# A four-layer decoder with cross-attention and a composed MLP: the first norm's two loads on separate semaphores, two column products for four, and GpSimd's weight splits at another wait

## What is computed

```python
for i in range(4):                                   # x: 2048 tokens x 256
    h = layer_norm(x, ln1_g[i], ln1_b[i])            # (x - m) * rsqrt(v + eps) * g + b
    # heads 0-3: windowed softmax attention; heads 4-7: q = softmax(q), k = elu(k) + 1,
    # ctx = running sum over buckets of k^T v / sum(k), out = q @ ctx
    x = x + self_attention(h, Wq[i], Wk[i], Wv[i], Wo[i], bo[i])
    h = layer_norm(x, ln2_g[i], ln2_b[i])
    x = x + gelu(h @ W1[i] + b1[i]) @ W2[i] + b2[i]
x = layernorm(x0 + x)                                # x0: the input
x = layernorm(x + cross_attention(x, ctx_1024, Wq, Wkv, Wout, bout))
vals, idx = top_k(logits, 32)                        # twice, for fc1 and fc2, of 64 primitives
w = softmax(vals)
W = einsum('k,kir,kro->io', w, A[idx], B[idx])       # the composed weights
x = layernorm(x + gelu(x @ W_fc1) @ W_fc2)
```

## Time and profile before

| | us |
|---|---|
| median of 3 runs | 959.26 |
| lowest, highest | 958.53, 959.52 |
| the profiled execution, its own time | 958.49 |
| its span, first to last instruction | 956.3 |
| TensorE busy with products | 944.4 |
| VectorE busy | 673.6 |
| ScalarE busy | 611.8 |
| GpSimd busy | 480.2 |

### The profile page before, as it was taken

The page is one execution under the profiler, slowest core; times in us unless marked ns, Lnnn a source line. Parts: engine busy times, 40 slices in busy tenths (PEclk is TensorE's granted clock), DMA queues, the critical chain, the costliest instruction groups (busy, mean ns, idle before and its releaser), DMA issues.

```text
span 956.3 us, 21341 instructions
## 1 busy us (share of the span) xinstructions
PE 944.4 (99%) x8394; PEld 815.6 (85%) x8394; DVE 673.6 (70%) x1529; ACT 611.8 (64%) x1389; POOL 480.2 (50%) x381
## 2 busy tenths in 40 slices
PE   7999999999999999999999999999999999999998
PEld 4688888888888889888888888888997889998997
DVE  7796868677777868696777678776662776666445
ACT  4777777686776867777768677686856345444220
POOL 3437375456826472775466367816247224006453
PEclk9999999999999999999999999999999999999999
DMA  6231000001110000021000003000028696820001
GB/s 211 72 108 45 2 17 2 8 11 58 33 45 19 2 1 19 1 89 45 10 9 1 18 2 84 4 2 7 2 57 204 137 205 143 181 46 1 23 23 45
DMA packets 71582, 47.56 MB, mean 50 GB/s; under 512 B 44511, under 2 KB 68159, under 8 KB 71487
## 3 DMA queue, kind: packets, MB, share of 16 engines
q1 hardware_dynamic: 71487, 46.27, 18.9%
HBM read 44.16 MB, written 2.10 MB: 48 GB/s over the span
## 4 chain that ended last, share of the span: by engine, by line
PE 94%; DVE 3%; ACT 1%; issue 1%; DMA 0%; POOL 0%; SPq 0%; POOLq 0%; DVEq 0%; ACTq 0%
PE F L1460 21%; PE F L1614 19%; PE A L1460 16%; PE A L1802 5%; PE A L1795 5%; PE A L1559 4%; PE A L1955 4%; PE A L1517 3%; PE F L1474 2%; PE A L1576 2%; PE A L1474 2%; PE F L1453 2%; PE A L1550 1%; PE A L1453 1%; PE A L1533 1%; PE A L1526 1%
## 5 line engine op out<-in xcount | busy, mean ns | idle before, releaser
L1460 PE MATMUL F<-xt,w 128*128 128x512 f32 x864 | 217.8, 400 | 0.2 <-ACT scratch L1211 0.2
L475 POOL TENSOR_TENSOR ht<-scratch,ht 128x512 fp32r<-128x512 f32 x128 | 176.2, 1397 | 29.4 <-ACT ht L1214 27.9
L1460 PEld LDWEIGHTS F<-xt,w 128*128 128x128 f32 x864 | 157.6, 188 | 38.2 <-issue 3.0
L1614 PE MATMUL F<-w,ht 128*128 128x256 f32 x1536 | 188.8, 282 | 0.0
L1614 PEld LDWEIGHTS F<-w,ht 128*128 128x128 f32 x1536 | 182.8, 188 | 5.3 <-issue 4.6
L463 POOL TENSOR_TENSOR rstd<-var,minus_half 128x4 f32<-128x4 f32 x32 | 37.6, 1173 | 176.4 <-DVE var L611 175.8
L1211 ACT ACTIVATE scratch<-F,b_now 128x512 f32<-128x512 f32 x128 | 87.6, 684 | 36.6 <-POOL ht L475 19.0
L1460 PE MATMUL A<-wa,xt 128*128 128x512 f32 x372 | 89.8, 397 | 0.0
L470 POOL TENSOR_TENSOR x<-x,vec_f 128x1024 f32<-128x1024 f32 x16 | 38.0, 2376 | 93.7 <-DVE scratch L631 93.7
L1214 ACT ACTIVATE ht<-scratch 128x512 fp32r<-128x512 f32 x128 | 80.9, 632 | 4.1
L1460 PEld LDWEIGHTS A<-wa,xt 128*128 128x128 f32 x372 | 69.0, 188 | 15.9 <-issue 0.2
(11 more groups left out here) (264 smaller groups left out, 2041.9 us busy)
## 6 DMA issues: line engine op xcount, KB each, us to landing
raw_f<-in_L_attn_W_dram SPq DMA_DIRECT2D x8, 1024.0 KB, 5.5
scratch<-in_L_ffn_fc_B_dram SPq DMA_DIRECT2D x32, 256.0 KB, 4.2
scratch<-in_L_ffn_fc_A_dram SPq DMA_DIRECT2D x32, 256.0 KB, 4.0
raw_f<-in_L_ffn_fc_A_dram SPq DMA_DIRECT2D x32, 64.0 KB, 3.4
scratch<-in_x_dram SPq DMA_DIRECT2D x1, 2048.0 KB, 10.1
raw_f<-in_L_ffn_fc_B_dram SPq DMA_DIRECT2D x32, 64.0 KB, 3.2
x<-in_x_dram SPq DMA_DIRECT2D x3, 512.0 KB, 3.7
out_dram<-x SPq DMA_DIRECT2D x3, 512.0 KB, 2.9
```

Source lines behind the costliest of these rows:

```text
L475: pool.tensor_tensor(ht[:, 1, m, :], hf[:, m % 2, :], ht[:, 0, m, :].bitcast(F32), ALU.subtract).then_inc(h_lo, 1)
L1460: last = pe.matmul(out, lhs(a, c), rhs(b, c), start=clear and k == 0, stop=k == len(total) - 1, skip_group_check=not clear)
L1614: last = pe.matmul(F[:, t % 2, 0:D], ht[:, a, c, P * t:P * t + P], w2[:, b, c, :], start=k == 0, stop=k == len(passes) - 1)
```

## The change

Three edits, and the renaming that they need.

1. The first norm's scale load counts a semaphore of its own, `first_scale_loaded`; the shift's load alone counts `vec_a_loaded`. The first `ln_centred` waits for the scale, and the first `ln_shifted` for the shift. To stay within the number of semaphores, the four loads for the cross-attention share two semaphores instead of having one each. `vec_count` corrects the later counts, which are 16 lower. TensorE, in front of everything else, runs six float32 products of `ones` with itself, 128 columns each, as soon as `ones` is written.
2. `top_columns` makes one product of 32 columns for each parity, which covers both sets.
3. GpSimd's first splits wait for `top_step` to reach 6 instead of for `top_w`, and the bias behind them additionally for item 1's `qsub_done`.

```diff
@@ sync
-            load_vec(sp, 0, 0)
+            for i, (row, loaded) in enumerate(((ln1_g, first_scale_loaded), (ln1_b, vec_a_loaded))):
+                sp.dma_start(vec_a[:, i, :], row[bass.ds(0, 1)].broadcast_to([P, D])).then_inc(loaded, 16)
@@ gpsimd
             pool.wait_ge(top_const, 8)
-            pool.wait_ge(top_w, 1)
+            pool.wait_ge(top_step, 6)
             split_wo(pool, 0)
             split_lo(pool, w1_pieces(), w1_hi, w1_ready, 0)
+            pool.wait_ge(qsub_done, 2)
             pool_bias(pool, 0, 0, 0)
@@ vector
+        def vec_count(i, l):
+            return 32 * l + (32, 16)[i == 0]
+
         def ln_centred(dve, i, n, p, l):
             vec, loaded = ((vec_a, vec_a_loaded), (vec_f, vec_f_loaded))[i]
-            dve.wait_ge(loaded, 32 * (l + 1))
+            if n == 0 and i == 0:
+                dve.wait_ge(first_scale_loaded, 16)
+            else:
+                dve.wait_ge(loaded, vec_count(i, l))
...
             ln_centred(dve, 0, 0, 0, 0)
+            dve.wait_ge(vec_a_loaded, vec_count(0, 0))
             ln_shifted(dve, 0, 0)
@@ tensor
+            pe.wait_ge(const_step, 1)
+            for _ in range(6):
+                pe.matmul(F[:, 1, 0:P], ones[:, :].broadcast_to([P, P]), ones[:, :].broadcast_to([P, P]), start=True, stop=True)
             pe.wait_ge(const_step, 8)
             pe_busy(pe, F[:, 1, :], 7)
...
                 for j in range(2):
-                    for f in range(2):
-                        last = pe.matmul(F[:, 0, 32 * j + 16 * f:32 * j + 16 * f + 16], ones64[:, :],
-                                         weighted[:, f, :].rearrange("i (k j) -> i j k", j=2)[:, j, :], start=True, stop=True)
+                    last = pe.matmul(F[:, 0, 32 * j:32 * j + 32].rearrange("p (f k) -> p f k", f=2), ones64[:, :],
+                                     weighted[:, :, :].rearrange("i f (k j) -> i j f k", j=2)[:, j], start=True, stop=True)
```

20 lines of the change are left out of this document (10 added, 10 removed).

## The result

| | before | after |
|---|---|---|
| median of 15 runs, us | 958.93 | 960.15 |
| lowest, highest | 957.81, 959.77 | 959.65, 962.52 |
| the profiled execution, its own time | 958.49 | 960.54 |
| its span | 956.3 | 958.4 |

The ratio, which goes by the means (958.83 and 960.52), is 1.0018, with a 95% interval of 1.0011 to 1.0025. The change makes the kernel slower, by 1.2 us of median and 1.7 us of mean; the forecast was 957.7, with a range of 956.7 to 959.2, which the result leaves at its upper end.

A forecast was written before the change was run, and what follows sets the result against it. TensorE was taken to bound the kernel, with the start's chain running through the shift's load. Gains of 1.38 us (part 1) and 0.2 (parts 2 and 3) made 1.6, from 959.26 to 957.7, range 956.7 to 959.2.

The forecast's parts named there:

- the landing: First norm: the scale's load lands 3.3 us after its issue, at 5.15, so centring starts at 5.62 to 5.75.
- Rival C: First norm: scale lands later or 1/std slows beside the centring; about 0.3 us gained in all, 959.0; chance 0.08.
- it keeps its four lengths: First norm: the four shifting steps take as long as before, starting at 7.4 to 7.55 instead of 8.82.
- Cost of the filler: 0: Start: the five dummy products behind 1/std take 1.1 us, end at 8.4 and cost nothing.
- rival D: Start: the clock falls in TensorE's pause of 1.0 to 1.6 us, slowing queries and tokens; 963.5; chance 0.04.
- rival B: Start: clock rises late, dummies hold the transposes, part 1 gains only 0.5 to 1.2 us; 957.9 to 958.6; chance 0.13.
- Part 3's bias: Behind the splits: item 1's subtraction saves 0.7 us, which L671 gives back by waiting for the bias.
- Rival A: Behind item 1's subtraction: VectorE keeps the 0.7 us, L671 not being held for the whole bias; 957.4; chance 0.13.

The follow-up runs named there:

- e2: Kernel before with part 3 alone: earlier splits, and the bias waiting additionally for item 1's subtraction; 960.64 us (kernel before: 958.49), ratio 1.0022.
- e7: Changed kernel with GpSimd's first splits cut into quarters of the columns, four times the instructions; 959.25 us (kernel before: 958.50).
- e11: e5 without the bias's wait for item 1's subtraction; 957.73 us (kernel before: 958.68).
- e13: e11 with GpSimd's three masks moved behind item 0's shifting; 957.21 us (kernel before: 958.60).
- e12: e6 with six more float32 products of 16 columns behind its six; 958.76 us (kernel before: 958.68).
- e6: Kernel before with only the six float32 products added at TensorE's start; 959.06 us, ratio 1.0007.
- e4: Kernel before with only the two column products for four; 958.01 us (kernel before: 958.49).
- e5: Changed kernel with GpSimd's splits behind `top_w` again and without the six float32 products; 957.59 us (kernel before: 958.50).

## Why the prediction was wrong

**The step that failed** is in part 3: "Beside the splits `top_weigh`'s tiny VectorE steps now run; TensorE asks for `top_w` only behind a dozen transposes, so I put that at 0, and at 0.3 us at most." It measured 2.1 us on VectorE and 1.54 on TensorE. e1, with this wait alone put back, is level with the kernel before, and e2, with part 3 alone, is 2.1 us slower. Two errors are in the sentence. The steps were sized by their own length, 0.14 and 0.19 us, and not by what stands beside them, 0.7 to 1.25 us long; the text applied the very reading that was needed to L671 in the same part, and there it came out right (0.99 for "about 1.0"). And the dozen transposes were named as cover but not measured: they leave 0.66 us. The Trainium skill (SBUF — State Buffer, "SBUF: two separate sides") has it that whichever of VectorE and GpSimd takes the shared pair of ports first holds it for its whole instruction, and names VectorE operations in a 2-port performance mode and those with two SBUF inputs. The trace of after agrees: L801 and the two L804 end 0.02 to 0.05 us behind GpSimd's instructions. e7's L650, passed over by five pieces in a row, shows that the wait can be longer than the instruction that runs. L804 has one wide input and a scalar per partition, both in SBUF, and was held too.

**Part 1, the scale.** Right in mechanism, wrong in size in the changed kernel: 1.38 forecast, 0.35 measured. The term that failed is the landing "3.3 us later, at 5.15", one execution's figure taken as fixed. In the profiled executions with both loads on one semaphore it was 3.0 to 3.7 us (seven kernels), with its own 3.3, 3.4, 3.5, 3.6 and 3.7 in five and 4.4, 4.7, 4.8 and 4.9 in four. Rival C names just this, at 0.08. Whether an own semaphore makes late landings likelier, or whether the shared one only hid them (its count of 16 can be reached with packets of the other load), the runs don't settle. When the landing is early, 0.5 us more is lost to GpSimd's masks beside the shifting (2.19 us for 1.67; e11 against e13), which the prediction did not have, though it says "it keeps its four lengths". With them moved, e13 gives 1.44 us at the queries, the forecast's "1.4 us sooner". The start with both loads on one semaphore varies as well: the queries came at 11.98 to 13.17 us (six kernels; 14.00 in e12, which its extra products hold up), with the scale's own, SyncE's order kept, at 11.02 to 12.25 (nine).

**The six products.** "Cost of the filler: 0" was right at the start: in after the seven dummies end by 6.3 us, and the five took 1.24 us for the forecast 1.1. The six themselves took 2.9 us for the forecast 2.4, which moved the seven by 0.24 us and cost nothing. The pause behind them, 0.87 us in after and 1.52 in e6, left the granted clock up, so rival D's fall did not come. But the early rise is no work of theirs alone: e4 and e13 took 1.24 us without them, other kernels 1.5 to 2.3. Nor do they secure it: in e12 they run too, with twelve small ones behind them, and all twelve dummies stood at the lower level (5.28 us, 0.43 apart, to 11.2 us), which is what rival B describes. What the prediction left out is that twelve more records in front move every later step twelve records on in the packets that bring the instructions: 0.74 us in after, at a late packet. The prediction's own test, "TensorE idle anywhere between 110 and 700 us", is where it showed.

**Part 2** was right: 0.44 us on TensorE for the forecast 0.5, and VectorE takes 0.26 of it back in e4, near the forecast's 0.3, but at L1526 and not at L1550, where the prediction had looked for it.

**Part 3's bias** was right: the subtraction fell to 0.69, L679 rose to 0.99 and not to 0.83, and e11 against e5 shows 0.1 us between them. Rival A is refuted.

Sum in after: -0.35 + 1.70 - 0.41 + 0.24 + 0.89 = +2.07 us on the profiled executions, for -1.6 forecast. Of the 3.7 us between them, 1.70 are the step in part 3, 1.03 the landing (1.38 - 0.35), and 0.89 the stretch with the hole. The medians differ by 1.2 only; that the hole and the landing vary from run to run (after has 962.52 as its highest) fits with it, but only profiled executions show them. The base was a little high too: 959.26 was the median of three runs, and fifteen gave 958.93.

## What to carry to other kernels

When GpSimd's work is moved so that it runs beside VectorE, size each VectorE step there by the GpSimd instruction that it may meet, however small the step is, and by several of them where they follow without a pause, unless it reads only TensorE's banks; then work out in microseconds how much room its waiter leaves. A landing time read from one execution is a sample: look at the same load in several traces before a sum rests on it. Filler instructions at the start of a full engine are not free of effect 400 us later: compare the holes of the two traces, and where one stands without a releaser, count the engine's instructions up to it.

## What the runs showed of the hardware

- An instruction of 64 x 2 elements on VectorE took 0.72 us beside GpSimd for 0.14 alone; two of 64 x 32 took 1.90 for 0.38. Steps that read TensorE's banks kept their length beside the splits: 0.16 and 0.19 us for two small ones, 0.67 to 0.69 us for four copies of 128 x 512. Cut into pieces of 0.42 us without a pause between them, the splits held one step of 0.69 us for 2.66 us.
- TensorE stops when the packet with its next instructions is late. In six kernels the hole stood in front of the 4027th product, ended 2.4 to 2.9 us behind the late packet, lasted 0.17 to 1.22 us, and carried no releaser in the trace but "issue". In the thirteen without a hole that product came 3.1 to 6.0 us behind the packet. The Trainium skill (Runtime: NRT & Kernel Launch, "Instruction fetch mechanics") says that instructions are fetched in blocks of 16 KiB, 256 instructions each, by a DMA queue of the engine's own while it runs, and that the cost of crossing a block is mostly hidden. The 63 packets of 16 KB agree with the block, and the holes show a place where it isn't hidden.
- A second queue of loads made the first one's later: the tokens landed after 5.7 us instead of 2.9, and the kernel lost 2.6 us. The two small loads took as long as before from issue to landing (4.7 and 5.3 us).
- Five dummy products behind a pause took 1.24 to 2.29 us from kernel to kernel, 0.21 us from one to the next at the upper level of the clock and 0.43 at the lower, as the clock's rise fell before, into or behind them; nothing in these runs fixes which.
